# Dealing a pass's side work to its gaps by what else each gap holds

## The chip, the cores and the metric
One core of a Trainium2 chip runs the whole program. The metric is the device time of one execution in microseconds, as the median of three runs.

## The reference
A graph of 6250 nodes with 256 features and 106,250 directed edges, each node's loop among them, sorted by target. Two graph blocks are computed, with a residual and a layer norm around each:

```python
def _L0_gnn_ref(x, edge_index, W1, b1, gamma, beta, W2, b2):
    agg = jax.ops.segment_sum(x[src], dst, num_segments=x.shape[0])
    h = agg + x
    h1 = h @ W1 + b1
    mean = jnp.mean(h1, axis=0)
    var = jnp.mean(jnp.square(h1 - mean), axis=0)
    h1 = (h1 - mean) * jax.lax.rsqrt(var + BN_EPS) * gamma + beta
    h1 = jax.nn.relu(h1)
    return jax.nn.relu(h1 @ W2 + b2)
...
x = _layernorm(x + _L0_gnn_ref(...), axis=-1)
x = _layernorm(x + _L1_gnn_ref(...), axis=-1)
```

W1 is 256 x 1024 and W2 is 1024 x 256. The second block is three graph convolutions of width 256 with degree norms. So there are four aggregations over the edges, called passes 0 to 3 here.

## The kernel before, in words
The edges lie in 104 groups of 1024. A pass adds each edge's source row to the sum of its target, in `acc`, an accumulator with the nodes along the columns. Two methods share the groups.

**Gathered groups.** POOL gathers the 1024 source rows of a group by eight indirect DMAs into a slot of `ring` (L803; pass 0 has three slots). PE multiplies them with small masks (`group_strips`, L1103, matmuls at L1111), ACT copies the strips (L846), PE places them (`group_sums`, L1116, L1122), and VectorE adds them to `acc` (L1434) and makes the next group's masks (L1446, L1448). In pass 0 there are 72 such groups, in `SPARSE0`. The stretch of the program from one group's strips to the next's is a **gap**, number s for group s.

**Dense groups.** For 56 of the groups (448 tiles of 128 edges) small blocks of edge counts are built once, in pass 0. A **tile** is two or three VectorE instructions (`tile_hot`, L1484 for two tiles and L1486), one PE matmul into a PSUM bank (`build`, L1129) and one VectorE add (`add_tile`, L1501). After 16 tiles SP stores a block (800 KB, `store_block`, L679). Passes 1 to 3 use all blocks; pass 0 uses those of the first 256 tiles, four of them (a quad) at once: a block **step** multiplies one row block of `parts_d` (128 nodes, upper and lower halves of their bits, 256 KB, `load_row`, L703) with the widened counts (ACT, `widen0`, L871, from `quads`, which SP loads every seven steps, L698). On PE a step is `dense_step0` (L1132, matmuls at L1140). There are 4 x 49 = 196 steps. Row loads go through four buffers: SP issues row k + 3 when it comes to step k, and waits there for step k - 1.

```python
def load_row(k):
    b = k % NB
    wait(sp, s_step0, k - QUAD + 1)
    sp.dma_start(hbuf0[:, k % QUAD, :].bitcast(F32), parts[1][b * P:(b + 1) * P, :]).then_inc(s_row[k % QUAD], 16)
```

**W1 products.** When the sums of a chunk of 256 nodes are complete, PE transposes the chunk's own rows (`transpose_own`, L1154), VectorE adds them (`hidden_in`, L1533), and in the next gap PE makes four W1 products (`hidden`, L1167, eight records each). VectorE takes the statistics of each (L1539), ACT copies it out of PSUM (`keep_hidden`, L859), and after the fourth SP stores 1 MB (`store_hidden`, L630). Products use two PSUM banks in turn, so product p waits for the copy of product p - 2. `AT0[s]` lists the chunks that become complete in gap s.

**The order.** Every engine walks the same list, `PLAN` (L203 to L230): for each gap its strips, products, sums, own chunk and steps, with tiles dealt evenly between them. Behind each product stands one step, as long as the gap has steps. How many tiles and steps a gap gets is set ahead of it, by `spread` (L151):

```python
def spread(things, s0, s1):
    at = [[] for _ in range(NS0)]
    for n, t in enumerate(things):
        at[s0 + n * (s1 - s0) // len(things)].append(t)
    return at
```

Tiles 0 to 255 are spread over gaps 2 to 35, tiles 256 to 447 over gaps 36 to 70 (`TILES_AT`, L159), and the 49 steps of each of the four quads over gaps 12 to 23, 24 to 36, 37 to 49 and 50 to 62 (`STEPS0`, L165).

Of the kernel before, what the change touches and what calls it, by code (L numbers as in the profile page):

```python
# [51 lines left out]
def gnn_kernel(nc, x, src, dst, w1, b1, gamma, beta, w2, b2, wl, bl, out):  # L52
# [10 lines left out]
    NB = -(-N // P)  # L63
# [16 lines left out]
    NT, NS, MSG = T0[ND], S0[ND], max(NSG)  # L80
# [30 lines left out]
    def retire_plan(added, pairs):  # L111

        last = max(added)
        per = E / N
        ready = []
        for c in range(NCH + 1):
            lo, hi = c * CHUNK - MARGIN, (c + 1) * CHUNK + MARGIN
            ready.append((max(added[k] for k in range(NG) if k * GE < hi * per and (k + 1) * GE > lo * per), c))
        ready.sort()
        at, when = [[] for _ in range(last + 1)], 0  # L120
        for t, c in ready:
            when = max(t, when)
            when = min(when + (len(at[when]) > (when >= pairs)), last)
            at[when].append(c)
        return at
# [16 lines left out]
    TILES0 = QUAD * SUPER * HALFRUNS  # L142
# [5 lines left out]
    NS0 = len(SPARSE0)  # L148
# [8 lines that stand above are left out]
    BEGIN = 2  # L157
    TURN = NS0 // 2 if HALFRUNS else BEGIN
    TILES_AT = [a + b for a, b in zip(spread(range(TILES0), BEGIN, TURN), spread(range(TILES0, NT), TURN, NS0 - 1))]  # L159
    BUILT0 = [max(s for s in range(NS0) if t in TILES_AT[s]) for t in range(QUAD * SUPER - 1, TILES0, QUAD * SUPER)]  # L160
    READY0, END0 = (BUILT0[0] + 2 if HALFRUNS else 0), NS0 - 9
    WINDOW0 = [(READY0 + j * (END0 - READY0) // HALFRUNS, READY0 + (j + 1) * (END0 - READY0) // HALFRUNS)
               for j in range(HALFRUNS)]
    assert all(s0 >= b + 2 for (s0, s1), b in zip(WINDOW0, BUILT0))
    STEPS0 = [[] for _ in range(NS0)]  # L165
# [10 lines left out]
    for t in range(TILES0):  # L176
        k, j = DGROUPS[t // TILES], t // (QUAD * SUPER)
# [4 lines left out]
    AT0, AT1 = retire_plan(added0, NS0), retire_plan(added1, NSP - 4)  # L182
# [17 lines left out]

    PARTS_AT = [list(range(3 * s - 3, min(3 * s, NCH + 1))) if HALFRUNS and s else [] for s in range(NS0)]
    assert not HALFRUNS or (sum(PARTS_AT, []) == list(range(NCH + 1)) and not any(PARTS_AT[READY0 - 1:]))
    PLAN, owed = [], []  # L203
    for s in range(NS0):
        steps = iter(STEPS0[s])
# [35 lines left out]
    with ExitStack() as ctx:  # L241
# [69 lines left out]
        at = TOOK + 2 * WIN  # L311
# [14 lines left out]
        def part(region, n):  # L326
            u_at[0] += n
            return region[:, u_at[0] - n:u_at[0]]
# [21 lines left out]
        ts = part(vreg, 2 * BPC * D).rearrange("p (u b d) -> p u b d", u=2, b=BPC)  # L350
# [145 lines left out]
        for a in range(4):  # L496
            s = dict(slow_sems)
# [13 lines left out]
        for a in range(1, 4):  # L511
            s = fast[a]
# [1279 lines left out]
```

## Time and profile before

| | |
|---|---|
| Median of three runs | 2658.21 us (2651.41 to 2666.01) |
| Profiled execution | 2672.67 us |
| Its span | 2670.9 us |
| TensorE matmul, busy | 2242.3 us, 84 % |
| GpSimd (POOL), busy | 1670.9 us, 63 % |
| VectorE (DVE), busy | 1209.0 us, 45 % |
| ScalarE (ACT), busy | 1108.6 us, 42 % |
| DMA | 730.48 MB, 274 GB/s mean |
| Mean granted TensorE clock | 0.925 |

The span runs from the first instruction to the last. The profiled execution's own time stands beside the median since every duration below comes from that one execution. Pass 0 is about the first third of the span. Gap 20 begins at 295.3 us, gap 36 at 471.9, gap 63 at 758.1, gap 71 at 850.8. An engine's busy share is a mean over the stretch it is given for; a wait is put down to the last thing that ended it.

### The profile page before, as it was taken

The page shows a single profiled execution, that of the slowest core. Times are in us where ns is not written, and L with a number is a line of the kernel's source. Part 1 is how long each engine was busy: PE and PEld are TensorE (multiplying, and loading weights), DVE is VectorE, ACT ScalarE, POOL GpSimd, SP SyncE. Part 2 cuts the span into 40 slices and gives each one's busy share as a digit, 9 for nine tenths or more (in the row PEclk, how much of TensorE's full clock was granted, in tenths as well). Part 3 has the DMA queues.
Part 4 walks back from the last instruction along what each step waited for, and adds up shares of the span by engine and source line. Part 5 has one row for each costly group of instructions (what it writes and reads, how often), then busy time and mean ns, then how long its engine had stood idle before and what let it go on. Part 6 is the DMA issues. An engine that isn't in the chain of part 4 may idle for free.

```text
span 2670.9 us, 37106 instructions
## 1 busy us (share of the span) xinstructions
PE 2242.3 (84%) x12426; PEld 1652.9 (62%) x12426; DVE 1209.0 (45%) x3288; ACT 1108.6 (42%) x1676; POOL 1670.9 (63%) x1796
## 2 busy tenths in 40 slices
PE   3357888998878889899999789899987898999875
PEld 2124555666555778677777567677765666777653
DVE  6877777676676667113131340222222403232334
ACT  0458733343321555444444334444443343444320
POOL 5556767677673000677767647777775577777743
PEclk9569899999998999899999999999998999999987
DMA  4778888888864798889898988899998888988963
GB/s 130 240 267 264 285 281 293 280 294 293 288 227 137 257 331 299 261 299 323 298 316 294 300 278 267 270 310 306 316 311 289 264 272 275 300 294 296 301 226 112
DMA packets 400879, 730.48 MB, mean 274 GB/s; under 512 B 42967, under 2 KB 209943, under 8 KB 394787
## 3 DMA queue, kind: packets, MB, share of 16 engines
q0 software_dynamic: 86256, 250.72, 29.4%
q1 hardware_dynamic: 159731, 245.54, 26.7%
q10 hardware_dynamic: 154688, 231.65, 25.7%
q8 instruction: 109, 1.79, 0.3%
q14 instruction: 95, 0.78, 0.1%
HBM read 596.95 MB, written 130.77 MB: 272 GB/s over the span
## 4 chain that ended last, share of the span: by engine, by line
PE 56%; DMA 19%; DVE 12%; issue 6%; POOL 2%; ACT 2%; DVEq 2%; SPq 1%; ACTq 0%
PE ps L1275 30%; DMA hbuf<-parts_d 12%; PE ps L1167 6%; PE ps L1111 5%; PE ps L1177 4%; PE ps L1140 4%; DMA xs<-x_d 3%; DMA xs<-in_x_dram 3%; PE ps L1122 2%; DVE vreg L1501 2%; POOL ring L803 2%; PE ps L1259 2%; DVE vreg L1486 1%; PE ps L1129 1%; DVEq L1438 1%
## 5 line engine op out<-in xcount | busy, mean ns | idle before, releaser
L803 POOL DMA_INDIRECT ring<-table_d,idx x1152 | 1098.0, 953 | 495.0 <-issue 343.5
L1275 PE MATMUL ps<-wide,hbuf 128*128 128x512 f32 x4116 | 1052.1, 408 | 94.3 <-DMA hbuf<-parts_d 83.4
L1275 PEld LDWEIGHTS ps<-wide,hbuf 128*128 128x128 f32 x4116 | 769.8, 194 | 320.9 <-DMA hbuf<-parts_d 99.7
L984 ACT CAST wide<-abuf 128x1024 fp32r<-128x1024 uint8 (+1 forms) x588 | 553.4, 942 | 653.2 <-PE ps L1275 649.8
L803 POOL DMA_INDIRECT ring<-in_x_dram,idx x576 | 557.6, 968 | 279.7 <-issue 166.7
L1434 DVE TENSOR_TENSOR acc<-acc,ps 128x256 f32 x216 | 90.7, 420 | 584.6 <-PE ps L1122 569.8
L1111 PE MATMUL ps<-ring,hot 128*32 128x256 f32 x3456 | 251.5, 412 | 45.0 <-DVE place L1448 16.3
L1140 PE MATMUL ps<-wide,hbuf 128*128 128x512 f32 x784 | 242.2, 436 | 38.8 <-DMA hbuf<-parts_d 33.5
L1592 DVE SCALAR_TENSOR_TENSOR vreg<-ps,dinv,bias_bc 128x256 f32<-128x256 f32 (+1 forms) x147 | 64.5, 480 | 457.6 <-PE ps L1177 457.6
L1501 DVE TENSOR_TENSOR vreg<-vreg,ps 128x300 f32 x448 | 208.0, 464 | 88.9 <-PE ps L1129 44.6
L1129 PE MATMUL ps<-vreg 128*128 128x300 bf16 x448 | 143.1, 323 | 104.8 <-DVE vreg L1501 95.8
L1167 PE MATMUL ps<-acc,ureg 128*128 128x256 f32 (+1 forms) x800 | 195.3, 393 | 15.5 <-ACT ureg L859 15.0
L1140 PEld LDWEIGHTS ps<-wide,hbuf 128*128 128x128 f32 x784 | 143.1, 198 | 71.3 <-DMA hbuf<-parts_d 38.5
L1259 PE MATMUL ps<-ring 128*128 128x256 f32 (+1 forms) x784 | 176.6, 389 | 9.7 <-ACT ring L1002 6.5
L871 ACT CAST wide<-quads 128x512 fp32r<-128x512 uint8 x196 | 120.4, 618 | 149.5 <-PE ps L1140 145.9
L1111 PEld LDWEIGHTS ps<-ring,hot 128*32 128x32 f32 x3456 | 95.6, 115 | 139.4 <-issue 85.7
L1122 PE MATMUL ps<-place,strips 128*128 128x128 f32 x864 | 148.2, 298 | 36.0 <-ACT strips L846 35.9
L1167 PEld LDWEIGHTS ps<-acc,ureg 128*128 128x128 f32 x800 | 153.7, 202 | 39.9 <-issue 18.7
L1122 PEld LDWEIGHTS ps<-place,strips 128*128 128x128 f32 x864 | 134.2, 206 | 70.7 <-ACT strips L846 58.3
L1129 PEld LDWEIGHTS ps<-vreg 128*128 128x128 bf16 x448 | 44.5, 100 | 215.0 <-DVE vreg L1486 112.0
L1177 PE MATMUL ps<-wt_s,us 128*128 128x256 f32 (+1 forms) x588 | 160.6, 422 | 17.7 <-DVE us L1564 17.7
L1259 PEld LDWEIGHTS ps<-ring 128*128 128x128 f32 (+1 forms) x784 | 149.6, 194 | 36.5 <-DVE lnrec L1606 7.7
(162 smaller groups left out, 1736.2 us busy)
## 6 DMA issues: line engine op xcount, KB each, us to landing
hbuf<-parts_d ACTq DMA_DIRECT2D x84, 1024.0 KB
abuf<-ad_d ACTq DMA_DIRECT2D x63, 1024.0 KB
hbuf<-parts_d ACTq DMA_DIRECT2D x84, 768.0 KB
hbuf<-parts_d SPq DMA_DIRECT2D x196, 256.0 KB
parts_d<-vreg SPq DMA_DIRECT2D x72, 512.0 KB, 6.5
h_d<-ureg SPq DMA_DIRECT2D x23, 1024.0 KB
ureg<-h_d POOLq DMA_DIRECT2D x23, 1024.0 KB, 8.1
ad_d<-vreg SPq DMA_DIRECT2D x28, 800.0 KB, 4.5
```

The costliest lines, as they stand in the source:

```text
L803: pool.indirect_dma_start(out=ring[:, i % slots, j, :], out_offset=None, in_=table[0:N, :], in_offset=at).then_inc(g["rows"][i % slots], 16)
L871: act.copy(wide0[:, k % 2, :, :], one_block(quads[:, m % 2, :, :], m % DLOADS, bl)).then_inc(s_wide0, 1)
L984: act.copy(wide[:, k % 2, 0:ns, :], one_block(abuf[n % 2][:, 0:ns, :], n % DLOADS, bl)).then_inc(s_wide, 1)
L1111: ins = pe.matmul(ps[j * NARROW:(j + 1) * NARROW, 4, 0:D], hot[:, n % 2, j * EACH + e, :], ring[:, i % slots, j * EACH + e, :], start=(e = ...
L1122: ins = pe.matmul(ps[:, 5, h * WIN:(h + 1) * WIN], strips[:, i % 2, u * D + h * P:u * D + (h + 1) * P], place[:, n % 2, u, :], start=(u == ...
L1129: pe.matmul(ps[:, BUILDBANK + t % 2, 0:JW], lohot[:, t % TB, :], jhot[:, t % TB, :], start=True, stop=True).then_inc(s_bm, 1)
L1140: ins = pe.matmul(ps[:, 6 + h, :].rearrange("p (s n) -> p s n", n=P), hbuf0[:, k % QUAD, e * D + h * P:e * D + (h + 1) * P], wide0[:, k % ...
L1167: ins = pe.matmul(ps[:, pr % 2, e * CHUNK:e * CHUNK + n], w1_s[:, h, m * P:(m + 1) * P], acc[:, h, cols(c)], start=(h == 0), stop=(h == DH ...
L1177: ins = pe.matmul(ps[0:rows, 1, b * D:(b + 1) * D], us[:, u, h, b * P:b * P + rows], wt_s[:, a - 1, h, :], start=(h == 0), stop=(h == DH - 1))
L1259: ins = pe.matmul(ps[0:rows, 2 + u, b * D:(b + 1) * D], hT[:, u, m, b * P:b * P + rows], w2_s[:, m, :], start=(m == 0), stop=(m == HT - 1))
L1275: ins = pe.matmul(ps[:, 2 + 4 * q + h, 0:(n1 - 4 * q) * P].rearrange("p (s n) -> p s n", n=P), hbuf[:, bl, e * D + h * P:e * D + (h + 1) * P],
L1501: dve.tensor_tensor(to, to, product, ALU.add).then_inc(s_ba, 1)
```

## The change
A second dealer, `dealt`, takes what else a gap holds. Gaps get a share of the things that brings them to one level, though none counts less room than a quarter of a thing. For the tiles 256 to 447 what else a gap holds is 4.0 per chunk of products and 0.7 per own chunk. For the steps it is 7.5 per chunk of products and 0.3 per tile. Tiles 0 to 255 stay as they are; the windows of the quads stay too.

```diff
+    def dealt(things, s0, s1, held, each):
+
+        level = (sum(held[s0:s1]) + len(things) * each) / (s1 - s0)
+        room = [max(level - held[s], each / 4) for s in range(s0, s1)]
+        at, s, past = [[] for _ in range(NS0)], 0, room[0]
+        for n, t in enumerate(things):
+            while past < (n + 0.5) * sum(room) / len(things):
+                s += 1
+                past += room[s]
+            at[s0 + s].append(t)
+        return at
+
+    ROWS = [4.0 * len(AT0[s - 1] if s else []) + 0.7 * len(AT0[s]) for s in range(NS0)]
+    late = dealt(range(TILES0, NT), TURN, NS0 - 1, ROWS, 1.0)
+    TILES_AT = [ts if s < TURN else late[s] for s, ts in enumerate(TILES_AT)]
+    assert sum(TILES_AT, []) == list(range(NT))
+    PRODUCTS = [7.5 * len(AT0[s - 1] if s else []) + 0.3 * len(TILES_AT[s]) for s in range(NS0)]
+    STEPS0 = [[] for _ in range(NS0)]
+    for j, (s0, s1) in enumerate(WINDOW0):
+        for s, steps in enumerate(dealt(range(j * NB, (j + 1) * NB), s0, s1, PRODUCTS, 1.0)):
+            STEPS0[s] += steps
+
```

Counts worked out from the two programs (product gaps are those that hold the products of a chunk):

| gaps | kind | number | steps before, now | tiles before, now |
|---|---|---|---|---|
| 20 to 35 | product | 5 | 20, 3 | 37, 37 |
| 20 to 35 | other | 11 | 42, 55 | 83, 83 |
| 36 to 62 | product | 11 | 43, 3 | 62, 37 |
| 36 to 62 | other | 16 | 58, 100 | 87, 117 |
| 63 to 67 | product | 5 | 0, 0 | 27, 16 |
| 68 to 70 | other | 3 | 0, 0 | 16, 22 |

In the rows of the order below, L1111 and L1133 are strips, L1122 and L1144 sums, L1129 and L1151 a tile, L1140 and L1162 a step, L1167 and L1189 a product (the changed file's lines are 22 higher). PE in product gap 42, before:

```order
L1140 MATMUL ps<-wide,hbuf 128x512 x4
L1167 MATMUL ps<-acc,ureg 128x256 x4
L1129 MATMUL ps<-vreg 128x300
L1140 MATMUL ps<-wide,hbuf 128x512 x4
L1167 MATMUL ps<-acc,ureg 128x256 x4
L1129 MATMUL ps<-vreg 128x300
L1140 MATMUL ps<-wide,hbuf 128x512 x4
L1129 MATMUL ps<-vreg 128x300
L1167 MATMUL ps<-acc,ureg 128x256 x4
```

The same gap on PE in the changed program:

```order
L1133 MATMUL ps<-ring,hot 32x256 x8
L1151 MATMUL ps<-vreg 128x300
L1189 MATMUL ps<-acc,ureg 128x256 x8
L1151 MATMUL ps<-vreg 128x300
L1189 MATMUL ps<-acc,ureg 128x256 x4
L1151 MATMUL ps<-vreg 128x300
L1189 MATMUL ps<-acc,ureg 128x256 x4
L1144 MATMUL ps<-place,strips 128x128 x2
L1151 MATMUL ps<-vreg 128x300
```

The four steps are gone from between the products, and two products stand end on end.

SP's queue over gaps 42 to 46, before (L630 is the store of hidden values, L703 a row load, L698 a quads load, L679 a block store, L622 an own chunk):

```order
L630 DMA h_d<-ureg 128x2048
L703 DMA hbuf<-parts_d 128x512 x5
L698 DMA quads<-ad_d 128x4x1024
L703 DMA hbuf<-parts_d 128x512
L679 DMA ad_d<-vreg 128x6400
L703 DMA hbuf<-parts_d 128x512 x4
L622 DMA xs<-in_x_dram 128x2x256
L703 DMA hbuf<-parts_d 128x512 x2
L698 DMA quads<-ad_d 128x4x1024
L703 DMA hbuf<-parts_d 128x512 x3
L630 DMA h_d<-ureg 128x2048
```

The same stretch in the changed program:

```order
L652 DMA h_d<-ureg 128x2048
L720 DMA quads<-ad_d 128x4x1024
L725 DMA hbuf<-parts_d 128x512 x7
L720 DMA quads<-ad_d 128x4x1024
L725 DMA hbuf<-parts_d 128x512 x3
L701 DMA ad_d<-vreg 128x6400
L725 DMA hbuf<-parts_d 128x512 x4
L720 DMA quads<-ad_d 128x4x1024
L725 DMA hbuf<-parts_d 128x512 x6
L644 DMA xs<-in_x_dram 128x2x256
L725 DMA hbuf<-parts_d 128x512
```

Between the store of gap 42 and that of gap 46 there were 15 row loads, four of them for steps of gap 46; now over 20 stand there, all in gaps 43 to 45.

## Rows read from the trace of the kernel before
The columns of a row of busy times are: the stretch and its length in us, then busy us (and instructions) of PE, PEld (weight loads), DVE, ACT and POOL, the granted clock, the DMA share and GB/s.

**Rows 1.** Busy time by stage: gaps 20 to 35, and 36 to 62.
```profile
295.00:472.00 177.00, 150.68 (x870) 101.03 (x873) 136.64 (x396) 72.68 (x121) 122.90 (x129) 0.95 0.86 283
472.00:758.00 286.00, 251.24 (x1493) 179.51 (x1488) 195.99 (x562) 106.51 (x180) 197.04 (x206) 0.98 0.87 290
```
**Rows 2.** Instruction groups of 472 to 758 us (busy, mean ns, idle before, releasers).
```profile
L803 POOL DMA_INDIRECT ring<-in_x_dram,idx x206 | 197.0, 956 | 88.8 <-issue 60.3 <-PE ps L1111 28.5
L1140 PE MATMUL ps<-wide,hbuf 128*128 128x512 f32 x404 | 121.7, 428 | 22.0 <-DMA hbuf<-parts_d 18.7 <-DVE acc L1526 3.1
```
**Rows 3.** Busy time summed over the eleven product gaps of 36 to 62.
```profile
sum 162.74, PE 149.25 PEld 114.50 DVE 103.56 ACT 57.23 POOL 106.95; mean PE 13.57 PEld 10.41 DVE 9.41 ACT 5.20 POOL 9.72
```
**Rows 4.** The same, summed over the sixteen other gaps of 36 to 62.
```profile
sum 123.52, PE 102.13 PEld 65.19 DVE 92.69 ACT 49.43 POOL 90.17; mean PE 6.38 PEld 4.07 DVE 5.79 ACT 3.09 POOL 5.64
```
**Rows 5.** The same, the five product gaps of 20 to 35.
```profile
sum 68.57, PE 66.74 PEld 50.82 DVE 49.11 ACT 31.61 POOL 46.06; mean PE 13.35 PEld 10.16 DVE 9.82 ACT 6.32 POOL 9.21
```
**Rows 6.** The same, the eleven other gaps of 20 to 35.
```profile
sum 108.00, PE 83.51 PEld 49.97 DVE 87.39 ACT 40.64 POOL 76.51; mean PE 7.59 PEld 4.54 DVE 7.94 ACT 3.69 POOL 6.96
```
**Rows 7.** Timeline of PE in product gap 42 (start us, us, what).
```profile
548.75 1.89 PE L1167 MATMUL ps<-acc,ureg 128*128 128x256 f32 x8
550.48 0.29 PE L1129 MATMUL ps<-vreg 128*128 128x300 bf16 x1
550.51 1.19 PE L1140 MATMUL ps<-wide,hbuf 128*128 128x512 f32 x4
551.54 1.89 PE L1167 MATMUL ps<-acc,ureg 128*128 128x256 f32 x8
```
**Rows 8.** SP's DMA queue in gaps 43 to 45 (packets, MB, share of 16 engines).
```profile
q1 hardware_dynamic: 2544, 5.32, 66.9%
```
**Rows 9.** The same queue in gaps 47 to 49.
```profile
q1 hardware_dynamic: 2532, 5.30, 59.4%
```
**Rows 10.** The same queue in gaps 55 to 58.
```profile
q1 hardware_dynamic: 3657, 6.90, 64.7%
```
**Rows 11.** Timeline of SP at the start of gap 43 (559.66 us).
```profile
560.60 0.32 SPq L630 DMA_DIRECT2D h_d<-ureg  x1
```
**Rows 12.** SP's DMA queue in 472 to 758 us.
```profile
q1 hardware_dynamic: 27346, 55.52, 56.6%
```
**Rows 13.** Timeline of DVE: a tile with the compare for two.
```profile
405.20 0.41 DVE L1484 TENSOR_TENSOR vreg<-lot,vreg 128x256 bf16<-128x256 f32 x1
405.52 0.36 DVE L1486 TENSOR_SCALAR vreg<-vreg,keyt 128x300 bf16<-128x300 f16 x1
405.79 0.49 DVE L1501 TENSOR_TENSOR vreg<-vreg,ps 128x300 f32 x1
```
**Rows 14.** Timeline of PE in gap 67, which has products and no steps.
```profile
822.08 0.29 PE L1129 MATMUL ps<-vreg 128*128 128x300 bf16 x1
822.21 1.89 PE L1167 MATMUL ps<-acc,ureg 128*128 128x256 f32 x8
824.62 1.96 PE L1167 MATMUL ps<-acc,ureg 128*128 128x256 f32 x8 [0.52 <-ACT ureg L859]
```
**Rows 15.** Busy time in gap 64 (columns as in rows 1).
```profile
770.47:782.51 12.04, 10.12 (x63) 7.65 (x62) 9.46 (x27) 3.31 (x6) 9.19 (x10) 1.00 0.70 213
```
**Rows 16.** Busy time summed over the product gaps 63 to 67.
```profile
sum 70.95, PE 52.94 PEld 39.91 DVE 55.10 ACT 15.83 POOL 50.51; mean PE 10.59 PEld 7.98 DVE 11.02 ACT 3.17 POOL 10.10
```
**Rows 17.** The same, gaps 68 to 70.
```profile
sum 21.72, PE 14.07 PEld 6.57 DVE 19.08 ACT 1.70 POOL 9.06; mean PE 4.69 PEld 2.19 DVE 6.36 ACT 0.57 POOL 3.02
```
**Rows 18.** Timeline of PE in product gap 54.
```profile
682.50 1.23 PE L1140 MATMUL ps<-wide,hbuf 128*128 128x512 f32 x4 [4.17 <-DMA hbuf<-parts_d]
683.79 3.45 PE L1167 MATMUL ps<-acc,ureg 128*128 128x256 f32 x8
...
688.16 1.89 PE L1167 MATMUL ps<-acc,ureg 128*128 128x256 f32 x8
```
**Rows 19.** Instruction group of 295 to 472 us.
```profile
L1140 PE MATMUL ps<-wide,hbuf 128*128 128x512 f32 x249 | 77.9, 439 | 3.3 <-DMA hbuf<-parts_d 3.3
```

## The prediction
> **What bounds the kernel now.** The change touches pass 0 alone, so I read two stretches of it first: gaps 20 to 35 and 36 to 62 [rows 1]. They take 177 and 286 us. In them TensorE is busy 0.85 and 0.88 of the time, POOL 0.69, DMA 0.86 and 0.87, so no engine is plainly the bound. The instruction groups of the second stretch say what each waits for [rows 2]: POOL spends 197.0 us on 206 gathers and 60.3 us between them, so 1.25 us a gather and 10.0 us for a group of eight, and waits for PE only 28.5 us. PE's steps wait 18.7 us for rows of parts_d.
>
> Then I split the gaps in two kinds. A product gap follows a gap that takes an own chunk, and holds 32 W1 records; any other gap holds none. In gaps 36 to 62, eleven product gaps take 162.74 us with PE busy 149.25, and sixteen others take 123.52 us [rows 3, 4]. In gaps 20 to 35 it is five with 68.57 us and eleven with 108.00 us [rows 5, 6]. A product gap is a matter of PE (14.8 us against 7.7 us), and PE's timeline shows why [rows 7]: a product takes 1.73 us (548.75 to the tile at 550.48), a step 1.03 us (550.51 to 551.54), end on end.
>
> The others are not short of PE. In gaps 43 to 45, 47 to 49 and 55 to 58, SP's DMA queue q1 works 66.9, 59.4 and 64.7 % of the time of the 16 engines [rows 8 to 10], with the gathers' queue beside it. SP issues the 1 MB store of the products at 560.60, one microsecond into gap 43 [rows 11], and the next row loads stand behind it.
>
> **Prices.** q1 moved 55.52 MB in 56.6 % of 286 us [rows 12]: 161.9 us of all engines, 2.92 us per MB. So a row load (256 KB) is 0.77 us, a store of hidden values (1 MB) 3.06, a quads load (512 KB, one per seven steps) 1.53, a block store (800 KB, one per 16 tiles) 2.39. On PE a step is 1.03 us, and a tile 0.13 (822.08 to 822.21 in [rows 14]). On VectorE a tile is 0.9 us: the first compare, for two tiles, takes 0.32 up to the next, and from there to the end of the add it is 0.76 [rows 13].
>
> **The change, part by part.** Nothing is added or removed; work changes its gap.
>
> Gaps 36 to 62, product gaps. They lose 40 of 43 steps (41.2 us of PE) and 25 of 62 tiles (3.3 us). With the steps go waits that only steps have: 4.17 us for a row in gap 54 and the 1.6 us of half clock behind it [rows 18], and the 3.1 us for the adds of a finished quad [rows 2]. 162.7 - 41.2 - 3.3 - 4.2 - 1.6 - 3.1 = 109. One thing may come instead: a step between two products hides the older one's way through VectorE's statistics and ACT's copy. Gap 67 already has products without steps; one of its four waits 0.52 us for the copy [rows 14]. That would be 4 us in eleven gaps, less what the thinner tiles give back; I take 1 us (bounds 0 and 22: gap 64, with six tiles and an own chunk, takes 12.04 us [rows 15], eleven of those 132). **110 us**, 53 less.
>
> Gaps 36 to 62, the others. They get 42 steps more (58 to 100) and 30 tiles more (87 to 117). PE needs 42 x 1.03 + 30 x 0.13 = 47 us more, and is idle 21 us of them now (123.52 - 102.13). VectorE needs 27 us more and is idle 31. The queue matters more: it works 0.636 of the time in the ten gaps of [rows 8 to 10], so 78.6 us in all sixteen. Added: 42 rows 32.3, six quads 9.2, nearly two block stores 4.5, so 124.6 us of work. How fast q1 can go beside the gathers is the unknown. The highest stretch shown has 0.669 [rows 8], and with 0.67 these gaps take **186 us**, 62 more than now. Bounds: POOL's pace sets a floor of 27 x 10.0 = 270 us for the stretch, 160 for these gaps, and 0.594 as in [rows 9] gives 210. I take 0.67, since the queue will have work waiting all the time, as in [rows 8]. Row loads have only four buffers, so the DMA time that product gaps leave free can't be used ahead. Sum for the stretch: 110 + 186 = 296, **+10 us** (-16 to +46).
>
> Gaps 20 to 35. Tiles stay. The product gaps lose 17 of 20 steps, 17.5 us of PE, which would make 51 us of 68.6. But VectorE's 49.1 busy us stay, and statistics wait behind tiles there, so I take 57. The others get 13 steps: 13.4 us of PE into 24.5 idle, and 12.8 us of queue work. With q1 at 0.61 of their time now (an estimate, between 0.594 and 0.636) they would take (66 + 13) / 0.67 = 118 us by the queue, and 160 - 57 = 103 by POOL. The wait for rows was 3.3 us here [rows 19], so the queue isn't full yet; I take the middle, 111. Sum 168 for 176.6: **-9 us** (-16 to 0).
>
> Gaps 63 to 70. Five product gaps, 70.95 us [rows 16], lose 11 of 27 tiles, 9.9 us of VectorE; POOL is busy 50.5 us there, and VectorE's work on degrees stays, so some 6 us of it come out. The last three gaps are VectorE's (19.08 busy of 21.72 [rows 17]) and get 6 tiles, +5.4. Together **-1 us** (-5 to +5). Gaps 12 to 19 get two steps, which the waits there hide; at worst +2.
>
> Queues. On SP the rows stand behind the same stores, now 6 or 7 in a gap and none in most product gaps. On ACT the widening copies go with the steps; ACT is busy 0.37 of the stretch. POOL's order is unchanged, and nothing behind pass 0 moves.
>
> Sum: +10 - 9 - 1 = 0 us. The profiled execution took 2672.67 us (span 2670.9), 14.5 over the median of the three runs, 2658.21; I set the difference against the median: **2658 us**. A measurement of this kernel can tell about 0.5 %, 13.3 us, from no change.
>
> **Rivals.**
> 1. Faster: POOL alone stays the bound. Once the other gaps last 10 us, gathers and rows no longer crowd: DMA at 0.87 of 286 us is 249 us of work, and the stretch has 270. It takes q1 at 0.77 in the other gaps. Then 36 to 62 takes 270 (-16), 20 to 35 takes 160 (-16), the end -2: 2624. For it: the waits for rows are only 18.7 us now. Against: stores, quads and blocks come in lumps ahead of the rows, and no stretch shows over 0.67.
> 2. Slower: the row ring starves. Product gaps leave DMA time unused, and the others need all of it. At 0.594, gaps 36 to 62 take 110 + 210 = 320 (+34), gaps 20 to 35 keep half their gain: +29, 2687. It decides from a share of 0.63 down: 124.6 / 0.63 = 198, +22 there and over +13 in all. For it: [rows 9] has 0.594, and I take gap 54's 4.17 us wait for such a pile. Against: [rows 9] ends in a gap that had little to load.
> 3. Slower: the clock. Behind the 4.17 us wait the next product takes 3.45 us and a later one 1.89 [rows 18], the levels 1.2 and 2.4 GHz. The seven runs of other gaps, each with one such wait and its slow matmuls, some 3 us, make +21: 2679. Against: with 18.7 us of short waits the stretch keeps a granted clock of 0.98 [rows 1]. The Trainium skill (TensorE: Matmul & The Clock Gate, HAM oscillation) has it as a rule that bursts of matmuls with DMA waits between them are throttled anew each time. The trace agrees at that one place, and the rule speaks against this change if waits grow.
>
> **Chances.** The forecast (the queue between 0.64 and 0.70, 2645 to 2671) 0.42; rival 1, 0.32; rival 2, 0.18; rival 3, 0.08. So faster 0.32, same 0.42, slower 0.26. The range runs from rival 1 nearly to rival 2, 2624 to 2684; the likeliest case alone has 2645 to 2671.
>
> **What would show it.** Product gaps of 36 to 62 near 10 us (over 11: the copies are exposed). The others near 11.6 us with q1 at 0.67, PE waiting over 30 us for rows in the stretch. Rival 1 shows other gaps at 10 us and POOL never waiting. Rival 3 shows a clock under 0.9. The forecast is wrong if gaps 36 to 62 last under 280 or over 310 us.

## The result, and the profile after

| | before | changed |
|---|---|---|
| Median | 2659.18 us (10 runs) | 2683.21 us (10 runs) |
| Ratio, 95 % interval | | 1.009 [1.0072, 1.0109] |
| Profiled execution | 2672.67 us | 2681.57 us |
| Span | 2670.9 us | 2679.8 us |
| Gap 20 begins | 295.3 us | 299.2 us |
| Gap 36 begins | 471.9 us | 475.4 us |
| Gap 63 begins | 758.1 us | 786.0 us |
| Gap 71 begins | 850.8 us | 875.3 us |

The change is slower by 0.9 %. The forecast was no change, 2658 us; the time lies just inside the range, by the second rival's side. One of the changed kernel's ten executions took 2855.25 us at a granted clock of 0.774 and isn't in the ratio; without it the median is 2681.57 us. Pass 0 ends 24.5 us later (875.3 for 850.8), which is about the difference of the medians, 24.0. The two spans differ by only 8.9 us, because the profiled execution of before spent 1820.1 us behind gap 71 and the changed one 1804.5, on code that is the same; the first was 14.5 us over its median of three, as the prediction said.

Busy time by stage, gaps 20 to 35 and 36 to 62 of the changed kernel (columns as for [rows 1]):

```profile
299.18:475.40 176.22, 150.73 (x850) 99.67 (x849) 136.74 (x396) 70.74 (x115) 124.10 (x129) 0.92 0.83 273
475.40:785.98 310.58, 264.70 (x1507) 183.27 (x1507) 203.23 (x573) 112.25 (x183) 209.10 (x218) 0.96 0.83 277
```

The second stretch takes 310.6 us for 286. The mean busy share of DMA is lower than before in both (0.83 for 0.86 and 0.87), and the granted clock is a little lower too. The first stretch's length didn't change (176.2 us for 176.6).

The same six sums as before, in the order product gaps and others of 20 to 35, product gaps and others of 36 to 62, gaps 63 to 67 and gaps 68 to 70. They answer to [rows 5, 6, 3, 4, 16, 17]:

```profile
sum 53.71, PE 51.87 PEld 39.18 DVE 45.49 ACT 23.21 POOL 39.14; mean PE 10.37 PEld 7.84 DVE 9.10 ACT 4.64 POOL 7.83
sum 122.51, PE 98.87 PEld 60.49 DVE 91.25 ACT 47.52 POOL 84.96; mean PE 8.99 PEld 5.50 DVE 8.30 ACT 4.32 POOL 7.72
sum 114.30, PE 106.90 PEld 83.12 DVE 75.82 ACT 32.91 POOL 77.22; mean PE 9.72 PEld 7.56 DVE 6.89 ACT 2.99 POOL 7.02
sum 196.28, PE 157.80 PEld 100.15 DVE 127.40 ACT 79.34 POOL 131.88; mean PE 9.86 PEld 6.26 DVE 7.96 ACT 4.96 POOL 8.24
sum 64.18, PE 50.50 PEld 38.49 DVE 47.27 ACT 13.83 POOL 38.64; mean PE 10.10 PEld 7.70 DVE 9.45 ACT 2.77 POOL 7.73
sum 25.11, PE 15.71 PEld 6.75 DVE 22.97 ACT 2.08 POOL 8.54; mean PE 5.24 PEld 2.25 DVE 7.66 ACT 0.69 POOL 2.85
```

The product gaps gave 63 us back (14.9 and 48.4), and the others took 87 (14.5 and 72.8). Each gap 36 to 62 with products now takes 10.4 us, each other 12.3.

The mean of a stretch hides how DMA is used in the two kinds of gap. Here are its shares in gaps 36 to 62, with the busy time summed over the gaps of a kind (q1 is SP's queue, q0 the gathers'; the total takes in two small queues):

| gaps 36 to 62 | q1 | q0 | all DMA |
|---|---|---|---|
| product, before | 85.2 us, 0.524 | 49.4 us, 0.304 | 0.832 |
| product, changed | 40.1 us, 0.351 | 36.1 us, 0.316 | 0.672 |
| other, before | 76.7 us, 0.621 | 35.6 us, 0.288 | 0.912 |
| other, changed | 124.8 us, 0.636 | 56.3 us, 0.287 | 0.925 |

So the gaps that got the steps had their DMA engines nearly full already, and kept them so for 73 us more, while the product gaps now leave a third of theirs unused.

What PE's steps and POOL waited for in 475 to 786 us, and the steps in 299 to 475, answering to [rows 2, 19]:

```profile
L825 POOL DMA_INDIRECT ring<-in_x_dram,idx x219 | 210.0, 959 | 100.3 <-issue 62.0 <-PE ps L1133 38.3
L1162 PE MATMUL ps<-wide,hbuf 128*128 128x512 f32 x414 | 126.2, 441 | 31.4 <-DMA hbuf<-parts_d 31.2
...
L1162 PE MATMUL ps<-wide,hbuf 128*128 128x512 f32 x232 | 74.0, 452 | 11.6 <-DMA hbuf<-parts_d 11.6
```

The waits for rows went from 18.7 to 31.2 us and from 3.3 to 11.6. POOL waits for PE more than before (38.3 us for 28.5), so it isn't the bound. PE's timeline in gaps 43 and 45 shows the waits and what follows them:

```profile
562.79 2.07 PE L1162 MATMUL ps<-wide,hbuf 128*128 128x512 f32 x4 [2.37 <-DMA hbuf<-parts_d]
...
584.50 1.19 PE L1162 MATMUL ps<-wide,hbuf 128*128 128x512 f32 x4 [0.19 <-DMA hbuf<-parts_d]
...
589.76 3.81 PE L1162 MATMUL ps<-wide,hbuf 128*128 128x512 f32 x8 [3.92 <-DMA hbuf<-parts_d]
```

The record of a step lasts 1.2 us, but 2.07 behind the 2.37 us wait, and those of two steps 3.81 behind the 3.92 us one. The granted clock is 0.50 from 562.79 to 564.86 us and 0.54 from 589.76 to 592.00: the clock is at its lower level, 1.2 GHz, for nearly all of that. SP's timeline shows when the rows were asked for:

```profile
553.44 0.32 SPq L652 DMA_DIRECT2D h_d<-ureg  x1
553.81 0.43 SPq L725 DMA_DIRECT2D hbuf<-parts_d  x1
556.83 0.32 SPq L701 DMA_DIRECT2D ad_d<-vreg  x1
557.20 3.82 SPq L725 DMA_DIRECT2D hbuf<-parts_d  x4
...
583.06 0.32 SPq L701 DMA_DIRECT2D ad_d<-vreg  x1
583.43 0.43 SPq L644 DMA_DIRECT2D xs<-in_x_dram  x1
583.90 3.16 SPq L725 DMA_DIRECT2D hbuf<-parts_d  x4
587.17 0.37 SPq L720 DMA_DIRECT2D quads<-ad_d  x1
```

A row is asked for when PE is three steps short of it. At 553.8 SP has issued one and gets no further in its list until a block is complete (556.83); only then does it come to the next row. At 583 a block store and an own chunk go out just ahead of the rows, 1 MB between a request and its use. The order shown ahead of the prediction for this stretch doesn't have the first of these block stores with its five rows; in the trace 20 row loads stand in gaps 43 to 45.

How long a row takes from its issue to its landing is in this row of the same stretch; the row below it is gap 45, where PE waits 3.92 us (columns as for [rows 1]):

```profile
hbuf<-parts_d SPq DMA_DIRECT2D x100, 256.0 KB, 5.6
...
577.84:593.64 15.80, 11.69 (x60) 7.46 (x59) 7.54 (x21) 4.70 (x9) 7.76 (x8) 0.89 0.99 335
```

The median is 5.6 us. The other gaps now hold 6.25 steps in 12.3 us, so three steps are 5.9 us, and nothing is left for a request that goes out late. In a product gap of before the steps stood 2.79 us apart (548.75 to 551.54 in [rows 7]), three of them 8.4; in the others of before they stood 2.1 us apart (58 in 123.5 us), three of them 6.4, but only 3.6 to a gap. Over gap 45 DMA is 0.99 busy, so its late rows also stand behind other transfers.

The share of SP's queue q1 in gaps 43 to 45, 47 to 49 and 55 to 58, which answer to [rows 8 to 10], and then in 60 to 62 and in all of 475 to 786 us, for [rows 12]:

```profile
q1 hardware_dynamic: 4936, 9.44, 66.8%
...
q1 hardware_dynamic: 4342, 8.15, 63.1%
...
q1 hardware_dynamic: 5818, 9.96, 67.1%
...
q1 hardware_dynamic: 3248, 6.59, 53.0%
...
q1 hardware_dynamic: 28215, 56.81, 53.1%
```

In the ten gaps of the first three the queue reaches 0.658 (81.2 of 123.4 us), with the gathers' queue at 0.26 to 0.28 beside it. In gaps 60 to 62 it doesn't.

### The profile page after: what moved, and what is told of

It reads as the page before. It is cut to its first block, busy times and chain, and to the rows that moved or that the text cites. A ratio compares the mean times of both kernels' runs of the same rounds, so it can differ in the third digit from the quotient of the medians.

```text
span 2679.8 us, 37106 instructions
## 1 busy us (share of the span) xinstructions
PE 2244.9 (84%) x12426; PEld 1647.3 (61%) x12426; DVE 1212.4 (45%) x3288; ACT 1112.2 (42%) x1676; POOL 1674.3 (62%) x1796
## 4 chain that ended last, share of the span: by engine, by line
PE 55%; DMA 24%; DVE 11%; issue 5%; ACT 2%; DVEq 1%; SPq 1%; POOL 0%; ACTq 0%
PE ps L1297 31%; DMA hbuf<-parts_d 16%; PE ps L1189 5%; PE ps L1133 5%; PE ps L1162 4%; PE ps L1199 4%; DMA xs<-in_x_dram 3%; DMA xs<-x_d 2%; PE ps L1144 2%; DVE vreg L1523 2%; PE ps L1151 1%; DVE lnst L1625 1%; DMA h_d<-ureg 1%; DVE vreg L1624 1%; PE ps L1176 1%
## 5 line engine op out<-in xcount | busy, mean ns | idle before, releaser
L1162 PE MATMUL ps<-wide,hbuf 128*128 128x512 f32 x784 | 244.9, 447 | 58.7 <-DMA hbuf<-parts_d 55.5
L1133 PE MATMUL ps<-ring,hot 128*32 128x256 f32 x3456 | 249.3, 409 | 44.0 <-DVE place L1470 16.8
L1151 PE MATMUL ps<-vreg 128*128 128x300 bf16 x448 | 145.4, 329 | 97.3 <-DVE vreg L1523 90.2
L1162 PEld LDWEIGHTS ps<-wide,hbuf 128*128 128x128 f32 x784 | 147.2, 206 | 94.4 <-DMA hbuf<-parts_d 67.5
L1189 PE MATMUL ps<-acc,ureg 128*128 128x256 f32 (+1 forms) x800 | 190.7, 388 | 12.8 <-ACT ureg L881 12.1
L1133 PEld LDWEIGHTS ps<-ring,hot 128*32 128x32 f32 x3456 | 95.0, 114 | 138.1 <-issue 82.8
L1144 PE MATMUL ps<-place,strips 128*128 128x128 f32 x864 | 146.4, 295 | 36.3 <-ACT strips L868 36.2
L1189 PEld LDWEIGHTS ps<-acc,ureg 128*128 128x128 f32 x800 | 148.7, 197 | 44.8 <-issue 19.4
L1151 PEld LDWEIGHTS ps<-vreg 128*128 128x128 bf16 x448 | 45.0, 101 | 210.3 <-DVE vreg L1508 109.5
L1144 PEld LDWEIGHTS ps<-place,strips 128*128 128x128 f32 x864 | 132.0, 203 | 68.8 <-ACT strips L868 57.2
```

Source lines behind the costliest of these rows:

```text
L1133: ins = pe.matmul(ps[j * NARROW:(j + 1) * NARROW, 4, 0:D], hot[:, n % 2, j * EACH + e, :], ring[:, i % slots, j * EACH + e, :], start=(e = ...
L1144: ins = pe.matmul(ps[:, 5, h * WIN:(h + 1) * WIN], strips[:, i % 2, u * D + h * P:u * D + (h + 1) * P], place[:, n % 2, u, :], start=(u == ...
L1151: pe.matmul(ps[:, BUILDBANK + t % 2, 0:JW], lohot[:, t % TB, :], jhot[:, t % TB, :], start=True, stop=True).then_inc(s_bm, 1)
L1162: ins = pe.matmul(ps[:, 6 + h, :].rearrange("p (s n) -> p s n", n=P), hbuf0[:, k % QUAD, e * D + h * P:e * D + (h + 1) * P], wide0[:, k % ...
L1189: ins = pe.matmul(ps[:, pr % 2, e * CHUNK:e * CHUNK + n], w1_s[:, h, m * P:(m + 1) * P], acc[:, h, cols(c)], start=(h == 0), stop=(h == DH ...
```

## The experiments

Theory Q is that the row loads can't keep up in the gaps without products. Q' is its later form, written ahead of the last runs: a lead of three steps is too short there, and DMA to spare doesn't help. Their rivals are that the dealt tiles cost (T), or that engines do: exposed copies, the clock. The chips differ: on some, the kernel before took 2658 to 2660 us, on two 3068 and 3092. On one of the two the profile of e1 shows 234 GB/s where before had 274. I call these two slow chips. Ratios are always to the kernel before on the same chip, and I draw on the other chips where I can.

**The changed kernel once more (e5).** No edit.

> The changed kernel itself, beside the ones below on one chip. Theory Q (the row loads of the other gaps wait for SP's queue): ratio to before about 1.009, on a chip with slower DMA 1.009 to 1.015.

2677.78 us, 1.0086 [1.0057, 1.0115], with 308.4 us in gaps 36 to 62 (310.6 the first time). The result stands.

**One part of the change alone (e1, e13, e17: steps; e2, e16, e18: tiles).** Steps only:

```diff
-    late = dealt(range(TILES0, NT), TURN, NS0 - 1, ROWS, 1.0)
-    TILES_AT = [ts if s < TURN else late[s] for s, ts in enumerate(TILES_AT)]
```

Tiles only: the lines of `PRODUCTS` and behind it are left out, and `STEPS0` is spread as before.

> Only the steps are dealt by what a gap holds; tiles 256 to 447 stay spread evenly. Theory Q (the loss is the row loads: product gaps leave DMA time unused, the other gaps ask for more than SP's queue brings): nearly the whole loss stays, ratio to before 1.007 to 1.012, row waits of PE in gaps 36 to 62 about 31 us as in the changed kernel. Rival T (the tiles piled into the other gaps make them long): the loss halves, ratio 1.002 to 1.005.

> Only the tiles 256 to 447 are dealt; steps stay spread evenly. Theory Q: no loss, ratio 0.997 to 1.001; product gaps 0.3 us shorter each, gaps 63 to 70 together 3 us shorter as in the changed kernel. Rival T: ratio 1.004 to 1.007.

On a slow chip: steps 1.007 [1.0045, 1.0095], tiles 0.9977 [0.9955, 0.9999].

> Steps dealt, tiles even, four row buffers, once more on a chip like that of the first timing. Theory Q' (a row is asked for only three steps ahead of its use, and in a dense run of steps its way through the queue takes longer than three steps; DMA rate to spare doesn't help): ratio 1.007 to 1.012, the whole loss of the change. Rival T (the tiles): 1.002 to 1.005.

> Tiles dealt, steps even, four row buffers, on a chip like that of the first timing. Two runs disagree: alone it had 0.9977 on the slower chip, and with six buffers it had 0.998 where six buffers alone had 0.9912, as if the tiles cost 0.7 %. If dealing the tiles alone costs (product gaps stay PE's at 13 us, and the other gaps get VectorE's work on top of their steps): 1.002 to 1.008. If not: 0.997 to 1.000.

On a slow chip again: 1.0003 [0.9975, 1.0031] and 0.9935 [0.9907, 0.9963]. Two timings of one kernel differ between the slow chips by more than their intervals, and none of the last two lies in a range that was expected. They tell only the sign of the difference between the two parts.

> Steps dealt, tiles even, four row buffers. The two times it ran it stood on the chip whose before takes 3070 to 3090 us, with 1.007 and 1.000. On a chip like that of the first timing Theory Q' expects 1.007 to 1.012 and row waits of PE of about 30 us in gaps 36 to 62; rival T 1.002 to 1.005.

> Tiles dealt, steps even, four row buffers; 0.998 and 0.994 on the slower chip. On a chip like that of the first timing Theory Q' expects 0.995 to 1.000; rival T 1.004 to 1.007.

On a chip like the first: steps **1.0127** [1.0098, 1.0156], tiles **1.0027** [1.0006, 1.0048]. POOL's and the steps' rows of gaps 36 to 62, first of e17, then of e18:

```profile
L823 POOL DMA_INDIRECT ring<-in_x_dram,idx x221 | 212.3, 961 | 107.7 <-issue 62.4 <-PE ps L1131 45.2
L1160 PE MATMUL ps<-wide,hbuf 128*128 128x512 f32 x421 | 128.8, 445 | 42.6 <-DMA hbuf<-parts_d 41.7 <-ACT wide L891 0.7
```

```profile
L1156 PE MATMUL ps<-wide,hbuf 128*128 128x512 f32 x408 | 125.7, 434 | 9.7 <-DMA hbuf<-parts_d 6.9 <-DVE acc L1542 2.7
```

The steps alone make the whole loss or more, with 41.7 us of row waits. Why there are more of them than with the tiles dealt too, no run shows. The tiles alone cost a little, which I had not expected, and the sums of e18 for the product gaps and the others of 36 to 62 say where:

```profile
sum 152.50, PE 144.80 PEld 112.28 DVE 81.55 ACT 54.11 POOL 100.18; mean PE 13.16 PEld 10.21 DVE 7.41 ACT 4.92 POOL 9.11
sum 148.65, PE 112.82 PEld 67.40 DVE 119.14 ACT 54.17 POOL 103.86; mean PE 7.05 PEld 4.21 DVE 7.45 ACT 3.39 POOL 6.49
```

25 tiles fewer shorten the product gaps by 10.2 us, 0.4 each; 30 more lengthen the others by 25.1 us, 0.84 each. That is nearly VectorE's whole price of a tile, 0.9, though VectorE was idle a quarter of the time there before and is a fifth of it in e18. What PE's tile matmuls wait for in gaps 36 to 62, before and in e18, shows how:

```profile
L1129 PE MATMUL ps<-vreg 128*128 128x300 bf16 x149 | 44.9, 301 | 7.2 <-DVE vreg L1501 6.9
...
L1145 PE MATMUL ps<-vreg 128*128 128x300 bf16 x155 | 47.1, 304 | 28.8 <-DVE vreg L1517 28.8
```

PE waits 28.8 us for VectorE's adds of earlier tiles, for 6.9. The two parts don't add: 1.27 and 0.27 % against 0.9 % together; in the changed kernel PE's tiles wait 7.1 us only, presumably since the steps make the same gaps longer.

**A milder deal (e3).**

```diff
-    PRODUCTS = [7.5 * len(AT0[s - 1] if s else []) + 0.3 * len(TILES_AT[s]) for s in range(NS0)]
+    PRODUCTS = [2.5 * len(AT0[s - 1] if s else []) + 0.3 * len(TILES_AT[s]) for s in range(NS0)]
```

> As the change, but a chunk's products count 2.5 instead of 7.5 for the steps: product gaps get 3 steps, the others 4 to 5. Theory Q: the queue's demand in the other gaps rises by a tenth only, ratio 0.998 to 1.003. If any step taken from between products costs (exposed copies), the ratio is in proportion to the steps moved, about a quarter of the loss and more, 1.003 to 1.005.

1.0006 [0.9988, 1.0025], on a slow chip. It is in the range of theory Q, below the steps alone on the same chip (1.007), but it can't be told from no change.

**Six row buffers (e4, e11 with the change; e6, e14 without).** Rows are asked for five steps ahead:

```diff
+ROWBUFS = 6
...
-        hbuf0 = sb("hbuf0", [P, QUAD, HALVED * D], F32R)
+        hbuf0 = sb("hbuf0", [P, ROWBUFS, HALVED * D], F32R)
...
-                wait(sp, s_step0, k - QUAD + 1)
+                wait(sp, s_step0, k - ROWBUFS + 1)
...
-                        if n + QUAD - 1 < NSTEP0:
-                            load_row(n + QUAD - 1)
+                        if n + ROWBUFS - 1 < NSTEP0:
+                            load_row(n + ROWBUFS - 1)
```

> The changed kernel with six row buffers instead of four, so five rows are loaded ahead and product gaps can load two more of them. If the waits are bursts (a store or a block ahead of the rows in one queue), PE's row waits in gaps 36 to 62 fall from 31 us to under 18 and the ratio to before is 1.001 to 1.005. If the queue's rate over the whole run of gaps is the limit, two more rows save at most 1.5 us of queue time at each of seven runs, 10 us, ratio 1.005 to 1.007. If it is the clock or the tiles, nothing changes, 1.009.

> The kernel before with six row buffers. Theory Q: it has 19 us of row waits in gaps 36 to 62 and 3 in 20 to 35, and the deeper ring takes some 10 of them: ratio 0.995 to 0.999. If the ring's depth helps only the changed order, 1.000.

> The changed kernel with six row buffers once more, since the first time stood beside no run of the changed kernel and on a chip with slower DMA. Bursts in one queue: 1.001 to 1.004. Rate alone: 1.005 to 1.007. Theory Q lets the deeper ring give the changed order no less than it gives the order before (0.9 %): then 0.999 to 1.001.

> The kernel before with six row buffers, beside the next run. Theory Q': 0.990 to 0.994, as the first time, and 0.3 % or more slower than the changed kernel with six buffers (0.9874).

Without the change 0.9912 [0.9881, 0.9943]; on a slow chip 0.9987 [0.9958, 1.0016]. With the change on a slow chip 1.0019 [0.9996, 1.0042], which is the range for bursts, and on a chip like the first **0.9874** [0.985, 0.9898], 2622.24 us. On chips like the first both gains were larger than any that was expected; on the slow one the kernel before gained less than expected. The deal costs 0.9 % with four buffers. With six it is some 0.4 % faster than six buffers alone, but the two ran on different chips and their intervals overlap, so this is likely and not shown. The sums of e11 for the same gaps as above, 20 to 35 and 36 to 62, then those of e6 for product gaps and others of 36 to 62:

```profile
sum 54.65, PE 51.60 PEld 39.02 DVE 46.44 ACT 25.16 POOL 41.46; mean PE 10.32 PEld 7.80 DVE 9.29 ACT 5.03 POOL 8.29
sum 109.04, PE 92.32 PEld 56.58 DVE 90.19 ACT 47.63 POOL 82.62; mean PE 8.39 PEld 5.14 DVE 8.20 ACT 4.33 POOL 7.51
sum 112.30, PE 105.34 PEld 81.86 DVE 77.53 ACT 32.38 POOL 83.11; mean PE 9.58 PEld 7.44 DVE 7.05 ACT 2.94 POOL 7.56
sum 165.15, PE 148.69 PEld 96.86 DVE 123.31 ACT 79.77 POOL 123.81; mean PE 9.29 PEld 6.05 DVE 7.71 ACT 4.99 POOL 7.74
...
sum 154.42, PE 147.78 PEld 113.29 DVE 99.82 ACT 56.67 POOL 108.46; mean PE 13.43 PEld 10.30 DVE 9.07 ACT 5.15 POOL 9.86
sum 119.67, PE 98.56 PEld 63.67 DVE 98.57 ACT 50.02 POOL 89.37; mean PE 6.16 PEld 3.98 DVE 6.16 ACT 3.13 POOL 5.59
```

The stage row of e11 for gaps 36 to 62, and what POOL and the steps wait for there:

```profile
453.60:731.00 277.40, 253.98 (x1507) 178.68 (x1506) 200.84 (x573) 112.10 (x183) 206.87 (x217) 0.97 0.91 307
```

```profile
L826 POOL DMA_INDIRECT ring<-in_x_dram,idx x217 | 207.9, 958 | 70.8 <-issue 65.2 <-PE ps L1134 5.6
L1163 PE MATMUL ps<-wide,hbuf 128*128 128x512 f32 x412 | 120.0, 431 | 2.9 <-DMA hbuf<-parts_d 2.7
```

The product gaps are as long as with four buffers (54.7 and 112.3 us for 53.7 and 114.3), the others 45 us shorter. Row waits are 2.7 us for 31.2, DMA is at 0.91 and 307 GB/s. The deal and the work are the changed kernel's, so the buffers make the difference, and they make it in two ways. In the product gaps DMA is busy 0.810 for 0.672, q1 51.7 us for 40.1: they take over work that stood in the others, whose DMA time falls from 181.6 to 160.5 us. At the changed kernel's share of 0.925 this alone would bring the others from 196.3 to 173.5 us. The rest, 8 us, is that their share rises to 0.972, q1's to 0.673. This split is an estimate from the two profiles; it takes the two for independent.

POOL waits for PE 5.6 us only: the stretch is at POOL's pace, 10.3 us a gap. But so it nearly is with six buffers and no deal: e6 takes 274.1 us for it, against 277.4. In gaps 36 to 62 the deal gains nothing even with six buffers; what e11 has over e6 is in gaps 20 to 35 (163.7 us for 173.9) and 63 to 70 (88.0 for 94.4).

**Half the bytes of the rows (e7 with the change, e8 without).** From the fifth row on only the upper halves are loaded; the products of the lower halves use stale rows.

```diff
+                part = HALVED * D if k < QUAD else D
-                sp.dma_start(hbuf0[:, k % QUAD, :].bitcast(F32), parts[1][b * P:(b + 1) * P, :])
+                sp.dma_start(hbuf0[:, k % QUAD, 0:part].bitcast(F32), parts[1][b * P:(b + 1) * P, 0:part])
```

> The changed kernel with row loads of half their bytes after the first four: only the upper halves are loaded, and the lower halves in the products are stale, so the output differs. 25 MB less on SP's queue in pass 0. Theory Q: the loss against the same edit of the kernel before (next run) vanishes: the two ratios to before lie within 0.3 % of each other. Rival (the loss is of the engines: clock, exposed copies, tiles): this one is 0.7 % or more slower than the next.

> The kernel before with the same halved row loads. Theory Q: it gains a part of its own row waits, up to 20 us, ratio 0.990 to 0.997, while the changed kernel with this edit gains 40 us or more.

0.9991 [0.9961, 1.0022] and 0.9965 [0.9935, 0.9994]. The distance between the two orders falls from 0.9 to 0.26 %, as expected; the changed kernel gained 26 us by it, not the 40 expected. So halving the traffic does less for the changed order than two more buffers, which take none of it away. The profile of e7 shows this in the others of 36 to 62: they take 181.0 us, DMA is busy only 0.840 of it (152.0 us of work for 181.6), and PE still waits 20.0 us for rows in the stretch. The rate of the DMA engines is thus not the whole limit: with a lead of three steps rows come late also where DMA has time.

**The 1 MB stores in ACT's queue (e12).**

```diff
                     if what == "hidden":
                         keep_hidden(fast[0], n, pr)
+                        if pr == HP - 1 and n < NCH - 1:
+                            store_hidden(act, fast[0], n)
```

with the same two lines taken out of SP's list.

> The changed kernel with the 1 MB stores of hidden values issued by ACT into its own queue instead of SP's, four row buffers. If rows wait because they stand behind the store in one queue: row waits of PE in gaps 36 to 62 fall by a third or more and the ratio to before is 1.002 to 1.006. If only the rate of the 16 engines counts: 1.008 to 1.010.

1.0048 [1.0028, 1.0067]. By its ratio the first theory, but the profile doesn't bear it out: its gaps 36 to 62 take 310.5 us, as the changed kernel's do, with 29.3 us of row waits, where they should have fallen by a third. So this store's place in SP's queue isn't the cause. Pass 0 ends 4.6 us before the changed kernel's there, nearly all of it ahead of gap 20 (295.4 us for 299.2), and only 0.7 us before that of e5; where its 0.4 % come from stays open.

**Six buffers with parts of the deal (e9, e10, e15).** Tiles alone; tiles and the mild steps; steps alone.

> Tiles dealt, steps spread evenly, six row buffers. Theory Q, with the gains of the two single edits added (0.9977 and 0.9912): ratio to before 0.987 to 0.991. If the two save the same time, 0.991 and no better than six buffers alone.

> As the run before with, in addition, the steps dealt mildly (a chunk's products count 2.5). Theory Q: moving a quarter of the steps asks a tenth more of the queue in the other gaps, 0.003 worse than the run before, 0.990 to 0.995. If with a deeper ring dealt steps pay, it is better than the run before.

> Steps dealt, tiles even, six row buffers. Theory Q': with rows asked for five steps ahead, dealing the steps pays: 0.986 to 0.990, at or near the changed kernel with six buffers. If the gain of that kernel needs the dealt tiles too, 0.991 to 0.995.

0.998 [0.996, 1.0], 0.9924 [0.9896, 0.9951], and on a slow chip 0.9951 [0.9927, 0.9975]. The first was expected at 0.991 or less: with steps spread evenly the tiles cost with six buffers too. Its gaps 36 to 62 take 289.0 us against 274.1 in e6, and PE's tiles wait 28.6 us for VectorE, as in e18. The second has a ratio in its range and was expected to be worse than the first; it is better, and the full deal (0.9874, on the same chip) is better still. So beside dealt tiles, dealing more of the steps pays with five rows of lead; with three the steps were the loss. The third was expected at 0.986 to 0.990 and missed it; on its slow chip it was a little faster than six buffers alone beside it (0.9987), with intervals that overlap.

## Why the prediction was wrong

- **The others of 36 to 62** were forecast at 186 us and took 196.3. Their queue work was right: 124.6 us were added up, and q1 is busy 124.8 us in them. The term that failed is the rate, "I take 0.67, since the queue will have work waiting all the time, as in [rows 8]". It came to 0.636, hardly over the 0.621 of before, with all DMA at 0.925. Beside the gathers' 0.287 it needed DMA at 0.96. The queue doesn't have work waiting all the time, because a row is requested only three steps ahead: it was at 0.658 in ten gaps but 0.530 in gaps 60 to 62, and about half of the 15 us in which DMA isn't busy lies in the first 2 us behind a product gap (0.43 busy in gap 43), where the buffers are still full. With six buffers it reaches 0.673. The prediction named the four buffers as a reason that product gaps can't be used ahead, which the six buffers confirm (product gaps' DMA 0.672, then 0.810), and didn't see them as a reason for waits within a run of steps.
- **The others of 20 to 35** were forecast at 111 and took 122.5, the largest single error. The step that failed is "so the queue isn't full yet; I take the middle", between 103 by POOL and 118 by the queue. DMA was busy 0.910 in these gaps before, so they were nearly full; the 0.86 of [rows 1] is a mean with the product gaps. q1's work came to 75.2 us (79 were added up) at a share of 0.614, which gives the 122.5. PE's idle time there stayed (24.5, now 23.6 us) and took up none of the 13 steps; row waits went from 3.3 to 11.6 us in the stretch. So -9 us became 0.
- **The product gaps** of 36 to 62 came out at 114.3 us where 110 were forecast, and those of 20 to 35 at 53.7 where 57 were. PE's busy time in the first fell by 42.3 us for the 44.5 of the prices, and products without steps are not much exposed: 2.3 us of waits for the copies in the stretch. VectorE does not hold the second ones at 57.
- **PE's idle time.** "PE needs 42 x 1.03 + 30 x 0.13 = 47 us more, and is idle 21 us of them now" left room for half of the steps. It took up none: PE's idle time in these gaps is 38.5 us now (196.28 - 157.80). PE's busy time grew by 56 us and not 47. A part is the third rival's: at granted clocks of 0.96 and 0.98 the stretch spends some 13 us more at the lower level than before, an estimate from the two stage rows, which costs 7 us at most. The rule of the Trainium skill (TensorE: Matmul & The Clock Gate, HAM oscillation), that bursts with DMA waits between them are throttled anew, agrees with the waits of 2.4 and 3.9 us and the clock behind them.
- **"VectorE needs 27 us more and is idle 31"** isn't room either, though it can't be seen in the result alone: in e18 each tile moved costs the others 0.84 us. With dealt steps beside them no such cost shows (1.0127 and 1.009, on different chips).
- **Gaps 63 to 70** gave 3.4 us for the 1 forecast. Gaps 12 to 19 took 2.3 us for two steps, where nothing was in the sum, and 1.7 us came ahead of them, where the program is the same.

Together: +24 for +10 in the second stretch, 0 for -9 in the first, +2 and +2 ahead of it and -3 behind. Gaps 36 to 62 took 310.6 us, just over the 310 that was named as a sign that the forecast is wrong (308.4 in e5). The second rival named the mechanism, the starved row ring beside product gaps that leave DMA unused, and gave 2687; its price by a share of 0.594 overshot the 0.636, and it had the product gaps and the early gaps a little better than they were. The weight of 0.18 on it was the misjudgement: the first rival's "the waits for rows are only 18.7 us now" is a measure of the old order, in which the steps of product gaps stood 2.8 us apart.

The first rival describes the stretch once the lead is there: with six buffers gaps 36 to 62 run near POOL's pace. They do so with the deal and without it.

## What to carry to other kernels

Before work that is fed by DMA is packed more densely, read the DMA share of the gaps that are to take it, and not the mean of a stretch: here the mean was 0.87 and the gaps that got the steps stood at 0.91. Then compare the lead of the requests in time, buffers ahead times the new distance between uses (5.9 us here), with the time from issue to landing (5.6 us here). Buffers are also what lets a gap without such work load ahead for the others. Work levelled by the engines' busy time needs its buffers levelled with it: with four row buffers the deal cost 0.9 %; with six it didn't. But test the buffers alone as well: of the 1.3 % that deal and buffers bring together, 0.9 % come without the deal. An engine's idle time in a stretch is not room for more of its work while the waits that make it idle come per item.

## What the runs showed that I had not expected

- The program ran on chips with medians of 2658 to 2660 us and on two with 3068 and 3092. On the slower two, two timings of one kernel (steps alone, tiles alone, once on each) differed by 0.7 and 0.4 %, and every ratio with six buffers lay within half a per cent of 1. The changed kernel with four buffers was not run there.
- The matmul clock fell behind a wait of 2.37 us, with one of 0.70 a step before it (granted 0.50 behind it, a step at 2.07 us instead of 1.20); that is shorter than the 4.17 us in the profile of before.
- An engine that had been idle a quarter of the time (VectorE, in the others of 36 to 62) made them longer by nearly its full price of the added work (e18).
- With six buffers and no deal (e6) gaps 36 to 62 take 274.1 us, less than the changed kernel with six (277.4).
